# Recurrence: the context layer norm's root and reciprocal taken per token, on 128 partitions by four columns, and spread to the channels by products with the identity

## The reference, cut to what matters

```
def step(s, rkvw):                       # layer 0
    r_t, k_t, v_t, w_t = rkvw
    a = k_t[:, :, :, None] * v_t[:, :, None, :]
    out = jnp.einsum('bhk,bhkd->bhd', r_t, u * a + s)
    return (a + w_t[:, :, :, None] * s, out)

def _layer_norm(x, gamma, beta):         # layer 1, over the context's channels
    mu = jnp.mean(x, axis=-1, keepdims=True)
    var = jnp.mean(jnp.square(x - mu), axis=-1, keepdims=True)
    return (x - mu) * jax.lax.rsqrt(var + LN_EPS) * gamma + beta
a = _layer_norm(audio_kv, ln_gamma, ln_beta)
K = (a @ Wk.T)
V = (a @ Wv.T)
```

## Time and profile before

| | us |
|---|---|
| median of three executions | 5328.55 |
| the three | 5319.98, 5328.55, 5329.23 |
| the profiled execution | 5320.13 |
| its span in the trace | 5318.5 |
| mean granted clock of TensorE, share of full | 0.949 |
| stage of the recurrence, in the trace | 410 to 1330 |

### The profile page before, as it was taken

The page is one execution under the profiler, slowest core; times in us unless marked ns, Lnnn a source line. Parts: engine busy times, 40 slices in busy tenths (PEclk is TensorE's granted clock), DMA queues, the critical chain, the costliest instruction groups (busy, mean ns, idle before and its releaser), DMA issues. The chain is left out here.

```text
span 5318.5 us, 75415 instructions
## 1 busy us (share of the span) xinstructions
PE 4723.6 (89%) x28818; PEld 1691.3 (32%) x28818; DVE 3735.3 (70%) x4684; ACT 2931.1 (55%) x5418; POOL 2013.1 (38%) x912
## 2 busy tenths in 40 slices
PE   5886998998688799997899999997789999996899
PEld 2332444443233233332322222221333333331344
DVE  6768999998453677772499999994567777771421
ACT  3553444444232366664288888886326666665432
POOL 0116666665000388885000000000008888886000
PEclk9897999999799799999999999998899999998999
DMA  2334434343220433322211111111424232212100
GB/s 99 125 138 132 116 103 114 112 113 89 92 65 33 89 69 69 69 57 97 87 29 32 32 32 33 33 33 47 134 87 99 58 77 61 65 45 76 64 24 16
DMA packets 474865, 391.90 MB, mean 74 GB/s; under 512 B 175151, under 2 KB 372628, under 8 KB 474472
## 3 DMA queue, kind: packets, MB, share of 16 engines
q1 hardware_dynamic: 474496, 387.00, 26.6%
HBM read 246.50 MB, written 139.34 MB: 73 GB/s over the span
## 5 line engine op out<-in xcount | busy, mean ns | idle before, releaser
L2803 DVE TENSOR_REDUCE att_part<-att_scores 128x2 f32<-128x802 f32 x1024 | 953.4, 986 | 108.6 <-PE att_scores L2642 96.8
L2776 ACT ACTIVATE att_prob<-att_lower 128x512 f32<-128x512 f32 (+1 forms) x1664 | 883.5, 596 | 128.4 <-PE att_lower L2656 107.4
L3610 DVE TENSOR_REDUCE att_part<-att_scores 128x1 f32<-128x423 f32 x1280 | 675.8, 590 | 219.3 <-PE att_scores L3313 219.2
L3554 ACT ACTIVATE att_prob<-att_lower 128x512 f32<-128x512 f32 (+1 forms) x1088 | 563.3, 602 | 243.9 <-PE att_lower L3325 242.0
L3594 POOL TENSOR_TENSOR att_acc<-att_acc,att_prob 128x1024 f32<-128x1024 f32 (+2 forms) x240 | 671.1, 2796 | 51.8 <-ACT att_prob L3554 22.6
L2379 DVE TENSOR_REDUCE att_part<-att_scores 128x1 f32<-128x401 f32 x1024 | 515.4, 567 | 161.9 <-PE att_scores L2193 161.7
L1373 POOL TENSOR_TENSOR scan_z<-scan_r,scan_states 128x512 f32<-128x512 f32 x256 | 469.6, 1839 | 337.4 <-DVE scan_states L1450 323.2
L2671 PE MATMUL att_lower<-att_prob,att_v 128*32 128x256 f32 (+1 forms) x6144 | 523.6, 413 | 19.7 <-issue 19.7
L2318 ACT ACTIVATE att_prob<-att_scores 128x512 f32<-128x512 f32 (+1 forms) x832 | 430.8, 601 | 195.3 <-PE att_scores L2205 195.2
L2790 POOL TENSOR_TENSOR att_out<-att_sums_sb,att_spread 128x512 f32<-128x512 f32 x32 | 40.7, 1272 | 1164.1 <-DMA att_spread<-recips 1164.1
L2359 POOL TENSOR_TENSOR att_acc<-att_acc,att_prob 128x1024 f32<-128x1024 f32 (+2 forms) x176 | 450.2, 2558 | 68.8 <-ACT att_prob L2318 56.4
(11 more groups left out here) (431 smaller groups left out, 7896.4 us busy)
## 6 DMA issues: line engine op xcount, KB each, us to landing
v<-scan_val SPq DMA_DIRECT2D x96, 256.0 KB, 2.3
att_v<-v SPq DMA_DIRECT2D x32, 768.0 KB
att_spread<-recips SPq DMA_DIRECT2D x64, 256.0 KB
mix_plane<-in_mask SPq DMA_DIRECT2D x16, 800.5 KB, 6.5
att_k<-k1hi SPq DMA_DIRECT2D x32, 400.2 KB
att_k<-k3hi SPq DMA_DIRECT2D x32, 400.2 KB
scan_x<-in_ctx_t SPq DMA_DIRECT2D x12, 1024.0 KB, 5.7
o<-att_out SPq DMA_DIRECT2D x32, 256.0 KB, 2.0
```

Of the source, the lines that this page charges most:

```text
L2776: nc.scalar.activation(prob[g % NP][0:kw(kt), h, :], scores2[0:kw(kt), n % RING2, :], ACT.Exp).then_inc(exped, 1)
L2803: nc.vector.reduce_max(part[q % 2][:, :, ec, piece], scores1[:, bank["unit", p], :, 0:PIECE], AX.X).then_inc(reduced, 1)
L3554: nc.scalar.activation(prob[g % NP][0:kw(kt), h, :], scores2[0:kw(kt), n % RING2, :], ACT.Exp).then_inc(exped, 1)
L3610: nc.vector.reduce_max(part[q % 2][:, hc, piece:piece + 1], scores1[:, bank["piece", p], 0:PIECE], AX.X).then_inc(reduced, 1)
```

## The change

The mean of squares is no longer made for all partitions at once. Each 128 tokens of the total become the stationary operand, and one column of k["mean"] the moving one, four times: the result has tokens on the partitions and four columns. Root and reciprocal work on 128x4 (65x1 in a tail). Then a new group, "spread", multiplies the reciprocal, each column broadcast to 128, with the identity, four times: the result is again 128x512 with the same row on every partition, and ScalarE copies it to std. VectorE's multiplication uses that. The group order gets one entry more, "spread", one key group behind "std", of the same cost as "std".

```
--- before.py
+++ after.py
             if o == std_behind(t):
                 yield t, "std", 0
+            if o == std_behind(t) + 1:
+                yield t, "spread", 0
             yield t, "k3", o
...
-    if what in ("mean", "std"):
+    if what in ("mean", "std", "spread"):
         return 1.0 * t.n / KT
...
+        rowstd, rowinv = ph.sb("rowstd", [P, KT // P]), ph.sb("rowinv", [P, KT // P])
...
+                def square_means(t):
+                    nonlocal made
+                    if made >= CR:
+                        pe.wait_ge(drained, made - CR + 1)
+                    for j, wd in enumerate(t.width):
+                        ins = nc.tensor.matmul(psum[0:wd, made % CR, j:j + 1], total[1][:, j * P:j * P + wd], k["mean"][:, 0:1],
+                                               start=True, stop=True)
+                    ins.then_inc(product, 1)
+                    made += 1
+
+                def spread_rows(t):
+                    nonlocal made
+                    if made >= CR:
+                        pe.wait_ge(drained, made - CR + 1)
+                    for j, wd in enumerate(t.width):
+                        ins = nc.tensor.matmul(psum[:, made % CR, j * P:j * P + wd], rowinv[0:wd, j:j + 1].broadcast_to([wd, P]),
+                                               k["ident"][0:wd, 0:wd], start=True, stop=True)
+                    ins.then_inc(product, 1)
+                    made += 1
...
                         elif what == "std":
                             pe.wait_ge(totalled, 2 * t.t + 2)
-                            group([(k["mean"][:], total[what == "std"][:, 0:t.n])], n=t.n)
+                            square_means(t)
+                        elif what == "spread":
+                            pe.wait_ge(inverted, t.t + 1)
+                            spread_rows(t)
...
                 def drain_std(t):
                     if t.t:
+                        act.wait_ge(inverted, t.t)
+                    m = t.width[0]
+                    drain(rowstd[0:m, 0:len(t.width)], ACT.Sqrt, m=m, n=len(t.width), bias=k["eps5"][0:m])
+
+                def drain_spread(t):
+                    if t.t:
                         act.wait_ge(normed, t.t)
-                    drain(std[:, 0:t.n], ACT.Sqrt, n=t.n, bias=k["eps5"][:])
+                    drain(std[:, 0:t.n], ACT.Identity, n=t.n)
...
+                            if o == std_behind(t) + 1:
+                                yield when[t.t, "spread", 0] + 1
+                                drain_spread(t)
...
+                def invert(t):
+                    m = t.width[0]
+                    dve.wait_ge(drained, end(t.t, "std", 0))
+                    if t.t:
+                        dve.wait_ge(drained, end(t.t - 1, "spread", 0))
+                    nc.vector.reciprocal(rowinv[0:m, 0:len(t.width)], rowstd[0:m, 0:len(t.width)]).then_inc(inverted, 1)
+
                 def normalise(t):
                     n = t.n
-                    dve.wait_ge(drained, end(t.t, "std", 0))
-                    nc.vector.reciprocal(std[:, 0:n], std[:, 0:n]).then_inc(inverted, 1)
-                    dve.wait_ge(inverted, t.t + 1)
+                    dve.wait_ge(drained, end(t.t, "spread", 0))
                     nc.vector.tensor_tensor(xc[:, :, 0:n], xc[:, :, 0:n], bc(std[:, 0:n], C), ALU.mult).then_inc(normed, 1)
...
-                        yield when[t.t, "std", 0] + 2
+                        yield when[t.t, "std", 0] + 1
+                        invert(t)
+                        yield when[t.t, "spread", 0] + 2
                         normalise(t)
```

## The result

| | median us | range |
|---|---|---|
| before | 5328.31 | 5319.6 to 5332.95, 9 runs |
| after | 5344.74 | 5335.39 to 5356.54, 9 runs |

A forecast was written before the change was run, and what follows sets the result against it. VectorE and TensorE were taken to bound the recurrence in alternation. Tile gains of 17.0 us less 4.7 of smaller terms gave 12.3 us off: 5307.8 against the profiled execution, 5316 against the median; range 5297 to 5337.

The forecast's parts named there:

- The third rival: TensorE's f32 weight loads: none hidden, 3.0 us more per full tile, so slower, 5340; chance 0.16.
- The plan's shift: First value group of v3 one step later in eight tiles, delaying the affine VectorE's low half awaits: -1.5 us.
- Tile 4: Full tile where TensorE would wait 3.7 us for the reciprocal; booked at -0.5 us instead of a 3.1 gain.
- hidden by the wait for GpSimd's total: Tail tiles: TensorE's wait of up to 2 us is hidden by a following 3.29 us wait; tails booked at -0.4.
- The second rival: Handshake of TensorE and VectorE in each tile takes the gain: 1 us more per full tile, 5328; chance 0.24.
- the sum by tile: Recurrence tiles: each gains the smaller of 3.1 and TensorE's wait behind the reciprocal less 0.9; 17.0 us in all.
- 0.4 us on each of the 7 tiles: Gaining tiles: GpSimd's z, formerly beside the reciprocal, now runs beside a scan and lengthens it; -2.8 us together.
- The 9 us: Alternative contention cost if the port shared by VectorE and GpSimd locks exclusively: 7 x 1.3 us, gain 6 us less.

The follow-up runs named there:

- the experiment with their order: Changed kernel with VectorE's reciprocal put ahead of the low half of k2 in the four tail tiles: 5334.94 us, 1.0009 of before.
- the plan alone: Kernel before with its instructions, but every group at the step the changed kernel's plan gives it: 5331.74 us, 1.0000 of before.
- The short reciprocal alone: Kernel before with VectorE inverting only 4 of the 512 columns of std, nothing else touched: 5321.94 us, 0.9985 of before.
- the timed run with wide means: Changed kernel with the means of squares as products of 128 columns instead of one: 5334.39 us, 1.0023 of before.
- 1.0008 with the wide means: Changed kernel with the reciprocal ahead of k2's low half in tails and 128-column means of squares: 5331.38 us, 1.0008 of before.
- z cut short: Kernel before with GpSimd's z made over 64 of its 512 columns: 5261.22 us, 0.9880 of before.

## Why the prediction was wrong

**Right.** The prices: 0.16 us for the reciprocal (0.22 taken), 0.81 and 1.00 for means and spread (0.75 and 1.1), VectorE's busy time in the stage lower by 32.6 us ("about 35"). The third rival is refuted: the eight loads of f32 weights of the spread lie hidden, 1.00 us and not 2.5, and with them the sentence of the Trainium skill ("TensorE: Matmul & The Clock Gate", "The mechanism") that loads overlap only in other row groups doesn't hold in this trace; the same section also has a load pulled ahead when it goes to the background weight buffer, which would fit. That the third rival's 5340 lies nearest to the measured 5345 is a coincidence: its mechanism isn't there. The plan's shift cost nothing that can be measured (1.5 booked). Tile 4 came as it was read: TensorE waits 3.73 us, 3.7 forecast, and tile 0 2.85 us.

**Wrong, first step: "hidden by the wait for GpSimd's total".** The tails were priced at 0.4 us together; they cost 15 us by the experiment with their order. The forecast allowed a wait of up to 2 us there. That took the reciprocal at the step where it is due, one ahead of where the list of VectorE lets it come. The list stood in the kernel: an instruction with an early due step behind one with a late one is late. This is what turned a small loss into a measurable one. The second rival had the right mechanism, a tie in both directions, and the wrong place: "tile 4", where it costs nothing; it was priced at 1 us per full tile and costs some 4 in each tail (15 in four).

**Wrong, second step: the sum by tile, "the smaller of 3.1 and TensorE's wait less 0.9", 17 us.** The full tiles from 8 to 14, booked at 11.9 us together, gave 1.5 by the two profiles (65.1 to 65.2, 62.1 to 62.1, 59.7 to 60.2, 65.7 to 64.9, 62.1 to 61.4, 58.7 to 58.1), and tiles 1 and 5, booked at 5.5, took 2.3 us more than in before's trace (0.9 less than with the plan alone). The short reciprocal alone, without TensorE's 0.9, gave 8 us in all, where the same rule gives over 20. The sum took each wait of TensorE behind the reciprocal as time that VectorE could give back. With the short reciprocal these waits hardly shrank (54.7 to 52.7 us for z and the low half), since VectorE gives half of its time back beside GpSimd and waits in turn for broadcasts and for the affine. The forecast looked at VectorE's next wait only in tile 2, and took it as absent elsewhere because the trace of before shows none there.

**Wrong, third step: the size of the contention, "0.4 us on each of the 7 tiles".** It was taken from the scan (1.25 to 1.70 us). In the changed kernel the multiply went from 2354 to 2849 ns, 5.9 us in 12 tiles, the low halves of k took 3.3 more; with the short reciprocal alone it was 19 us. The scans, on which the forecast had put it, took no more at all (425.0 to 422.1 us). The 9 us that the prediction worked out by the Trainium skill's exclusive lock ("SBUF — State Buffer", "Who interferes with whom") and set aside are nearer than the 2.8 that it took.

**Missing: the clock.** One-column products were priced by their own time alone. By the traces they cost some 4 us more in tile 6, where TensorE stays at the lower level behind them; the timed run with wide means gave 7 to 8 us, not clear of its noise.

**Sum of what is shown.** Of 20 us the tails' order makes up 15. With that mended 1.0009 is left (1.0008 with the wide means), which is hardly told from 1: there VectorE's 8 us and TensorE's additional work cancel. The clock in tile 6 is seen in the traces; where the tails are mended first, the timed runs show nothing of it, and whether it makes up the rest of the 20 us is open.

## What to carry to other kernels

Before time on an engine is priced, look at what runs beside it on the engine that shares its port: here the reciprocal, with one operand from SBUF, was a free window for GpSimd, and its successors paid once it was gone. When a chain of small steps goes through three engines, read the order in which each engine's list lets them come in the shortest tile, not in the usual one: there one unrelated instruction ahead of a 0.15 us step held up TensorE for 5 us. And try the gain first by leaving the work out: the short reciprocal alone showed that with this order of the work some 8 us were to be had, before anything was paid for doing it elsewhere.

## What the runs showed of the hardware

Not expected were three things. GpSimd's addition of 128x512 takes 1.26 us beside VectorE's reciprocal and 3.31 us beside its multiply, which itself takes 3.11 us instead of 2.29 (its mean with z cut short): nearly as if one had run after the other. Behind eight f32 products of one column, started at the lower clock level, twelve products of 512 columns ran at that level still (0.43 us apart, granted clock 0.57 and 0.59 over 10 us in tiles 2 and 6), while behind the same products with 128 columns, started at the lower level too, the clock was at 1.00 in tile 6. And a logarithm and an exponential in turn on ScalarE brought a load of tables of 1.28 us each time, 32 in the stage, where the root alone had one.
